# Attention scores by two 64-row halves of the array, a new order of one attention step, and a router by column groups

## What is computed

```python
qh = (layernorm(x) @ Wq + bq), kh = (ctx @ Wk + bk), vh = (ctx @ Wv + bv)   # split in 16 heads of 32
attn = softmax(qh @ kh.T / sqrt(32))                                     # 128 keys per head
x = x + tanh(g_xattn) * ((attn @ vh) @ Wo + bo)
xf = layernorm(layernorm(x)) * ln_gamma + ln_beta
logits = clip(xf @ router_w.T); two best experts, softmax of the two
y = w3[e] @ (silu(w12[e] gate @ xf) * (w12[e] up @ xf))                   # for rows within capacity
x = x + tanh(g_ffn) * sum of the two experts' y, weighted
```

## Time and profile before

| | us |
|---|---|
| median of 3 runs | 2676.12 (2672.24 to 2676.25) |
| time of the profiled execution | 2672.94 |
| its span, first to last instruction | 2671.2 |
| attention stage within it | about 482, then some 14 until the first expert matmuls |
| busy PE / DVE / ACT / POOL in the span | 2599.4 / 1362.1 / 952.6 / 422.7 |
| mean granted clock of TensorE | 0.987 |

### The profile page before, as it was taken

One profiled execution on the slowest core, in us unless ns is written; L12 is line 12 of the kernel. 1 busy time (PEld: TensorE's weight loads), 2 busy tenths in 40 slices (PEclk: granted clock), 3 DMA queues, 4 the chain that ended last, 5 costly groups with the idle time before them and its releaser, 6 DMA issues.

```text
span 2671.2 us, 40600 instructions
## 1 busy us (share of the span) xinstructions
PE 2599.4 (97%) x14168; PEld 2313.1 (87%) x14169; DVE 1362.1 (51%) x2628; ACT 952.6 (36%) x2498; POOL 422.7 (16%) x399
## 2 busy tenths in 40 slices
PE   7999999699999999999999999999999999999998
PEld 6888887699998888889888788888888999989987
DVE  5888887444444444454444444444434444445555
ACT  6777776222223222232222322322223322233343
POOL 5556565200001000010000200100001100030030
PEclk9999999799999999999999999999999999999999
DMA  8422323321114011140110511221013211142142
GB/s 332 176 97 91 107 80 112 121 88 47 47 36 110 28 43 47 34 116 24 47 47 27 124 48 71 68 71 48 24 47 71 77 47 47 47 90 102 71 128 82
DMA packets 58994, 208.37 MB, mean 78 GB/s; under 512 B 8517, under 2 KB 8797, under 8 KB 50563
## 3 DMA queue, kind: packets, MB, share of 16 engines
q1 hardware_dynamic: 42242, 175.30, 18.2%
q0 software_dynamic: 16640, 31.69, 6.2%
HBM read 145.60 MB, written 67.70 MB: 80 GB/s over the span
## 4 chain that ended last, share of the span: by engine, by line
PE 88%; DVE 4%; issue 3%; ACT 2%; POOL 1%; DMA 1%; another core or an unknown queue 1%; DVEq 0%; SPq 0%; ACTq 0%; POOLq 0%
PE bank L1601 78%; PE bank L947 6%; ACT staged L493 1%; PE bank L1047 1%; PE bank L1607 1%; PE bank L1011 1%; PE bank L1022 1%; DVE before L828 1%; PE bank L1038 0%; DVE neg_max L703 0%; POOL expert_rows L422 0%; POOL staged L389 0%; DVE xT_lo L640 0%; DVE yacc L1541 0%
## 5 line engine op out<-in xcount | busy, mean ns | idle before, releaser
L1561 DVE TENSOR_TENSOR h<-silu,bank 128x384 f32<-128x384 f32 (+2 forms) x320 | 183.8, 574 | 828.0 <-PE bank L1601 818.3
L1601 PE MATMUL bank<-slotsT_hi,early_hi 128*128 128x384 f32 (+2 forms) x1280 | 445.9, 348 | 13.1 <-issue 11.6
L1601 PE MATMUL bank<-slotsT_hi,w_hi 128*128 128x384 f32 (+2 forms) x1280 | 442.3, 346 | 3.2 <-DVE w_lo L1502 3.2
L1601 PE MATMUL bank<-slotsT_hi,early_lo 128*128 128x384 f32 (+2 forms) x1280 | 443.0, 346 | 1.7 <-issue 1.7
L1601 PE MATMUL bank<-slotsT_lo,early_hi 128*128 128x384 f32 (+2 forms) x1280 | 443.5, 346 | 0.0
L1601 PE MATMUL bank<-slotsT_lo,w_hi 128*128 128x384 f32 (+2 forms) x1280 | 442.1, 345 | 0.0
L1601 PE MATMUL bank<-slotsT_hi,w_lo 128*128 128x384 f32 (+2 forms) x1280 | 440.9, 344 | 0.0
L1469 ACT CAST h_hi<-h 128x384 fp32r<-128x384 f32 (+2 forms) x320 | 169.2, 529 | 744.0 <-DVE h L1561 741.1
L1463 ACT ACTIVATE silu<-bank 128x384 f32<-128x384 f32 (+2 forms) x320 | 162.0, 506 | 725.6 <-PE bank L1601 725.0
L1411 POOL DMA_INDIRECT out_dram<-yout,token x63 | 97.9, 1554 | 1969.4 <-ACT yout L1455 1957.9
L1541 DVE TENSOR_TENSOR yacc<-bank,yacc 128x512 f32<-128x512 f32 x464 | 316.6, 688 | 168.8 <-PE bank L1601 167.9
(11 more groups left out here) (199 smaller groups left out, 3508.9 us busy)
## 6 DMA issues: line engine op xcount, KB each, us to landing
staged<-in_moe_w_dram SPq DMA_DIRECT2D x33, 1536.0 KB
raw<-in_moe_w_dram SPq DMA_DIRECT2D x32, 1536.0 KB
xrow<-expert_rows SPq DMA_DIRECT2D x42, 520.0 KB, 8.8
expert_rows<-zeros SPq DMA_DIRECT2D x40, 520.0 KB, 7.8
xin<-in_x_dram SPq DMA_DIRECT2D x17, 512.0 KB, 3.8
xres<-in_x_dram SPq DMA_DIRECT2D x15, 512.0 KB, 3.7
out_dram<-xres SPq DMA_DIRECT2D x15, 512.0 KB
staged<-in_L_xattn_Wq_dram SPq DMA_DIRECT2D x1, 1024.0 KB, 7.2
```

Source lines behind the costliest of these rows:

```text
L1561: nc.vector.tensor_tensor(h32[q % 2][:, 0:W], silu[q % 2][:, 0:W], UB[q % 2][:, 0:W], ALU.mult)\
L1601: last = nc.tensor.matmul(out_ap, st, mv, start=(at == 0), stop=(at == n - 1))
```

## The change

Scores: `scores(n, g, b)` now makes a whole group, both token tiles. Each product is cut in two by heads: half c holds HP = 2 heads, 64 rows of the queries and keys and 256 columns of keys, and goes to bank c. For each tile t three passes, each alternating between the halves: 12 matmuls of 64 rows, 128 stationary and 256 moving columns. So bank c holds both tiles of half the heads; the scores of group g+1 wait for all exps of group g. `maxima` and `exps` go by (g, c).

Router: `rwT` is padded with zeros to 32 columns per block of features. `router(blk)` makes 4 matmuls (stationary rwT, 32 columns; moving xnT, both tiles, 256 columns), one for each block of features, to 32 partitions each. `copy_parts` on ACT copies the 128 x 256 result to SBUF, and `logits_made` multiplies it with `pick_expert`, which sums the four parts: 2 matmuls of 8 columns.

Step: PE, ACT and DVE have their pieces in a new order. On PE: scores 0, `transposes_x`, `queries(n, 1)`, `probs_T(n-1, 2)`, scores 1, `heads(n-1, 0)`, `probs_T(n-1, 3)`, `queries(n+1, 0)`, scores 2, `turn_rows`, `heads(n-1, 1)`, `router`, `probs_T(n, 0)`, `logits_made`, `attention_out(n-1, 0)`, scores 3, `positions`, `attention_out(n-1, 1)`, `probs_T(n, 1)`. In step 0 both `values_made` stand ahead of scores 1. In the tail the ACT casts of expert weights come behind the last `second_exp`. The orders on POOL and SP stay.

```diff
+            HP = HG // 2
+            parts_bank = lambda blk: l_bank(blk)[:, TB:2 * TB]
+                    nc.gpsimd.memset(rwT[:, :, :], 0.0)
...
                     def exps(blk, idx):
-                        g, t = divmod(idx, 2)
+                        g, c = divmod(idx, 2)
                         act.wait_ge(max_ready, 2 * KD * blk + idx + 1)
                         if not isinstance(blk, int) or blk > 0:
-                            act.wait_ge(pt_ready, 2 * KD * (blk - 1) + idx + 1)
-                        for hh in range(HG):
-                            h = HG * g + hh
-                            ins = nc.scalar.activation(probs[:, t, h, :], S_BANK[t][:, hh * LKV:(hh + 1) * LKV], ACT.Exp,
-                                                       bias=neg_max[:, t, h:h + 1], accum_out=sums[:, t, h:h + 1])
+                            act.wait_ge(pt_ready, 2 * KD * (blk - 1) + 2 * g + 2)
+                        for t in range(2):
+                            for hh in range(HP):
+                                h, at = HG * g + HP * c + hh, (HP * t + hh) * LKV
+                                ins = nc.scalar.activation(probs[:, t, h, :], S_BANK[c][:, at:at + LKV], ACT.Exp,
+                                                           bias=neg_max[:, t, h:h + 1], accum_out=sums[:, t, h:h + 1])
                         ins.then_inc(exp_done, 1)
...
+                    def copy_parts(blk):
+                        act.wait_ge(parts_ready, blk + 1)
+                        if not isinstance(blk, int) or blk > 0:
+                            act.wait_ge(l_ready, blk)
+                        nc.scalar.copy(parts[:, :], parts_bank(blk)).then_inc(parts_copied, 1)
...
                             pT_first(n - 1, 2)
+                        if has(n, 0):
+                            exps(n, 2)
+                        if has(n, -1):
                             a_halves(n - 1, 0)
                         if has(n, 0):
-                            exps(n, 2)
                             exps(n, 3)
...
                             a_halves(n - 1, 1)
+                        if has(n, -2):
+                            copy_parts(n - 2)
...
+                    copy_parts(LAST - 1)
+                    rows_T(LAST, (0,))
+                    second_exp(LAST - 1)
+                    rows_T(LAST, (1,))
+                    copy_parts(LAST)
+                    second_exp(LAST)
                     act.wait_ge(raw_loaded[0], 16)
                     for i in range(NU):
                         nc.scalar.copy(unit(w12_hi, w3_hi, 0, i), raw_unit(0, i)).then_inc(w_hi, 1)
-                        if i == NU // 2 - 1:
-                            rows_T(LAST, (0,))
-                            rows_T(LAST, (1,))
-                            second_exp(LAST - 1)
-                    second_exp(LAST)
...
                     def maxima(n, idx):
-                        g, t = divmod(idx, 2)
+                        g, c = divmod(idx, 2)
                         dve.wait_ge(s_ready, 2 * KD * n + idx + 1)
-                        nc.vector.tensor_reduce(neg_max[:, t, HG * g:HG * (g + 1)],
-                                                S_BANK[t][:, :].rearrange("p (h t) -> p h t", h=HG),
+                        nc.vector.tensor_reduce(neg_max[:, :, HG * g + HP * c:HG * g + HP * (c + 1)],
+                                                S_BANK[c][:, :].rearrange("p (t h k) -> p t h k", t=2, h=HP),
                                                 AX.X, ALU.max, negate=True).then_inc(max_ready, 1)
...
                             recips(n, 0)
-                            maxima(n, 2)
                             q_rest(n, 1)
+                        if has(n, 1):
+                            x_rest(n + 1)
                         if has(n, -1):
                             pT_second(n - 1, 2)
-                        if has(n, 1):
-                            x_rest(n + 1)
-                        if has(n, 0):
-                            maxima(n, 3)
                         if isinstance(n, int) and n == 0:
                             values()
+                        if has(n, 0):
+                            maxima(n, 2)
+                            maxima(n, 3)
                         if has(n, -2):
                             rows(n - 2)
...
                         if has(n, 0):
                             maxima(n, 4)
+                            maxima(n, 5)
                         if has(n, 2):
                             stats_x(n + 2)
                         if has(n, 0):
-                            maxima(n, 5)
                             recips(n, 1)
...
                             a_rest(n - 1, 1)
+                        if has(n, 0):
+                            pT_second(n, 0)
                         if has(n, -2):
                             route(n - 2)
                         if has(n, 0):
-                            maxima(n, 6)
+                            recips(n, 2)
                         if has(n, 1):
                             q_rest(n + 1, 0)
                         if has(n, 0):
-                            recips(n, 2)
-                            pT_second(n, 0)
+                            maxima(n, 6)
                             maxima(n, 7)
...
-                    def scores(n, idx, b):
-                        g, t = divmod(idx, 2)
+                    def scores(n, g, b):
                         pe.wait_ge(q_lo, KD * n + g + 1)
-                        if not isinstance(n, int) or 2 * KD * n + idx >= 2:
-                            pe.wait_ge(exp_done, 2 * KD * n + idx - 1)
-                        passes(S_BANK[t][:, :], [((qT_hi[:, g, t * P:(t + 1) * P], qT_lo[:, g, t * P:(t + 1) * P]),
-                                                  (k_hi[b][:, g, :], k_lo[b][:, g, :]))]).then_inc(s_ready, 1)
+                        if not isinstance(n, int) or KD * n + g >= 1:
+                            pe.wait_ge(exp_done, 2 * KD * n + 2 * g)
+                        for t in range(2):
+                            for i, (qs, ks) in enumerate(((qT_hi, k_hi), (qT_hi, k_lo), (qT_lo, k_hi))):
+                                for c in range(2):
+                                    rows, keys_of = slice(c * HP * DK, (c + 1) * HP * DK), slice(c * HP * LKV, (c + 1) * HP * LKV)
+                                    last = nc.tensor.matmul(S_BANK[c][:, t * HP * LKV:(t + 1) * HP * LKV],
+                                                            qs[rows, g, t * P:(t + 1) * P], ks[b][rows, g, keys_of],
+                                                            start=(i == 0), stop=(i == 2))
+                                    if t == 1 and i == 2:
+                                        last.then_inc(s_ready, 1)
...
+                    def router(blk):
+                        pe.wait_ge(xnT_ready, 2 * blk + 2)
+                        for k in range(KD):
+                            last = nc.tensor.matmul(parts_bank(blk)[DK * k:DK * (k + 1), :], rwT[:, k, :], xnT[:, :, k, :],
+                                                    start=True, stop=True)
+                        last.then_inc(parts_ready, 1)
+
+                    def logits_made(blk):
+                        pe.wait_ge(parts_copied, blk + 1)
+                        for a in range(2):
+                            last = nc.tensor.matmul(l_bank(blk)[:, a * E:(a + 1) * E], parts[:, a * P:(a + 1) * P],
+                                                    pick_expert[:, :], start=True, stop=True)
+                        last.then_inc(l_ready, 1)
...
                             scores(n, 0, b_s)
-                            scores(n, 1, b_s)
+                        if has(n, 1):
+                            if has(n, -2):
+                                pe.wait_ge(x1_ready, 2 * (n - 2) + 2)
+                            transposes_x(n + 1)
```

More of the change, by code:

```diff
@@ L553, in step @@
                             exps(n - 1, 7)
[L554 to L556 removed]
+                        if not isinstance(n, int) or n > 0:
                             if has(n, 1):
@@ L1088, in step @@
                             queries(n, 1)
-                            if isinstance(n, int) and n == 0:
-                                values_made(0)
-                            scores(n, 2, b_s)
-                        if has(n, 1):
-                            if has(n, -2):
-                                pe.wait_ge(x1_ready, 2 * (n - 2) + 2)
-                            transposes_x(n + 1)
                         if isinstance(n, int) and n == 0:
+                            values_made(0)
                             values_made(1)
```

44 lines of the change are left out of this document (19 added, 25 removed).

## The result

The kernel after takes 2692.5 us in the median of four runs (2690.5 to 2696.5), against 2676.2 for the kernel before beside it: a ratio of 1.0063, 95% interval 1.0051 to 1.0075. The forecast was 2668 and the range ended at 2690: slower, by 16 us, instead of faster by 8.6. In the profiled execution the span is 2693.9 us (its time 2696.5, which is 4.0 above the median).

The account below looks back on a forecast made before the run. PE bounds the attention step (27.07 of 27.17 us), then DVE at 24.5. Step 0 +7.9, step 1 +0.3, steps 2 to 13 -14.2, step 14 -1.1, tail -1.5: -8.6 from 2676.1, so 2668 us; range 2655 to 2690.

Parts of the forecast that it names:

- the walk: One attention step laid out anew, engine by engine, with assumed durations; it closed at 25.95 us a step.
- steps 2 to 13: Twelve attention steps going from 27.08 to 25.9 us each: -14.2 us.
- Scores: PE's score passes in attention: a group takes 0.95 us, with 0.95 to 1.65 as bounds.
- rival 1: Score passes: loads of the halves in series, group 1.65, step 27.3, 2691 us; chance 0.25 together with rival 4.
- Router: Attention step: eight head-like passes, an ACT copy and four passes; -0.85 us on PE, +0.35 on ACT.
- The step: Period of the attention loop: 25.9 us, from DVE's 24.5, a longer stall of 0.25 and 1.2 of waits.
- The base: Old attention loop: steps 2 to 13 take 27.08 us each, with PE's row of work packed.
- The term of +7.9: Step 0: PE waits for norm_x(1) and its clock falls, so the first scores of step 1 finish 7.9 us later.
- Step 14 and the tail: End of the attention stage: -1.1 us in step 14, -1.5 in step 15 and the tail.
- DVE's stall: A small DVE addition lasting until POOL's normalisation ends: 0.25 us longer per step; without the stall, 25.0 a step.
- DVE waiting longer than 1 us for maxima at group 2 or 3: Attention step: a sign that the forecast is wrong, making the exp round the bound.
- Rival 3: Attention: the stall of L828 goes and step 0 stays warm, -23 us, 2654 us; chance 0.07.

Follow-up runs that it names:

- before_third: The kernel before, unchanged, run for its trace on chip D, which had no holds: 2673.1 us.
- after_fourth: The kernel after, unchanged, on chip D without holds: 2673.6 us, ratio to the kernel before 1.0015.
- after_third: The kernel after, unchanged, on chip C without holds: 2673.5 us, ratio to the kernel before 1.0014.
- swap_third: The kernel after with queries(n, 1) put back ahead of transposes_x(n + 1) in all steps, on chip E: 2665.7 us.
- swap0: The kernel after with queries put back ahead of the transposes in step 0 alone, on chip A: 2666.9 us.
- late_scatter: The kernel after with queries ahead of transposes in all steps and POOL's four indirect DMAs moved behind norm(n - 1, 3) of the next step: 2701.6 us.

## Why the prediction was wrong, point by point

The step of the prediction that failed is the walk's second and third line: "queries(n,1) ... ends at 5.65. The ACT half is done at 6.6". I gave PE's signal to ACT no time at all beyond the pass, though the row that I cited for the length of a q half, has 1.65 us of idle time before it with a releaser that is no instruction of the core, and the earlier trace rows has 1.46 us before maxima that had their scores. I read the second as DVE's slack and did not read the first. Both are holds. They are the largest part of the miss, not all of it. The two profiled executions, before and after, give the sum term by term (their spans differ by 22.7 us where the medians differ by 16, so the miss is 31 us here and 25 in the medians):

| stretch | forecast | measured | |
|---|---|---|---|
| up to the start of step 2 | +8.2 | +11.4 | 74.02 to 85.47 |
| steps 2 to 13 | -14.2 | +5.3 | 324.9 to 330.2 |
| step 14 to the first product of expert 0 (L1601, L1629) | -2.6 | +6.2 | 103.4 to 109.6 |
| the rest | 0 | -0.2 | |

The same three stretches without holds, on chip D (before_third and after_fourth): +8.8, -6.0 and +1.7.


- **Scores.** A group of 0.95, taken from the heads' row, measured 0.90. Right, and rival 1 (loads in series, 1.65) is false, although its time of 2691 is the one that was measured: a number that comes out is no proof of its mechanism.
- **Router.** Eight passes and four, on PE as forecast; hidden in the new layout.
- **The step.** 25.9 forecast. Without holds 26.1 (after_third: (400.31 - 85.80)/12 = 26.2 over the steps 2 to 13), so the walk was off by 0.2 to 0.3. With holds 27.7: +1.6. Of the 19.4 us missing in steps 2 to 13, 15.7 are holds (330.2 against 314.5 in after_third) and 3.7 the walk's own.
- **The base.** I took 27.08 a step for the old layout; 26.7 is what its work sets, and 0.4 to 0.5 is holds. So the gain per step on a chip without holds is 0.5 to 0.6, not 1.2, and does not make up for step 0: even there the change does not pay. The forecast was 0.3% faster, and it is 0.15% slower (2673.5 and 2674.6 us against 2671.4 and 2671.1; on chip D 2673.6 against 2672.5).
- **Step 0.** PE idle from 22.2 to 28.1 and a low clock behind it, as told: eight transposes of line 998 take 1.97 us there, at a granted clock of 0.50 (28.11 to 30.10), and 1.09 in the loop. Forecast for scores(1,0) was 56.6, measured 57.95. For the start of step 2 I had 74.02 + 8.2 = 82.2; it is 85.47, and 85.80 in after_third. The term of +7.9 was mis-sized. It compared the end of the first two score tiles of step 1, before and after (49.7 and 57.5); from start to start step 1 comes 57.95 - 46.84 = 11.1 later, and then takes 27.52 us instead of 27.18, the +0.3 that was forecast. So nothing behind the scores got back the 2 us between the two ways to compare, and 1.35 us come from the later start itself. Together the two terms should have been 11.4 instead of 8.2; the exchange in step 0 gives back 7 to 9 (step 2 starts at 76.9 in swap_third and swap0, at 83.4 to 85.8 in the kernel after).
- **Step 14 and the tail.** Forecast -2.6, measured +6.2, and without holds -0.6 to +1.7 (105.1, 107.4 and 107.3 us in the kernel after against 105.7 in before_third). Step 14 alone is right without holds (25.7 us, before 26.7). That the walk to the last norm would gain did not come: from the start of step 15 it takes 30.4 to 30.7 us, before 28.6 and 30.2. Why is not shown.
- **DVE's stall** moved as the walk had it: it is now the addition of 1 in line 848, 1.88 us, ending at 359.54 with POOL's norm(n, 2) at 359.51. It hits a tensor_scalar with one SBUF source as well as the addition of two in the earlier trace rows; without holds it is line 854, 1.21 us. It was not the cause of the miss (the walk had counted a stall of this length), though it makes up 0.5 of the 1.6 us by which a step with holds is longer than one without.
- **What I said would show it.** "DVE waiting longer than 1 us for maxima at group 2 or 3" did not come; DVE waits 2.34 us for the q half instead, at a place where the walk had 1.0. A tail longer by more than 1 us did come.
- **A sum.** Rival 3's -23 us gives 2653, not 2654; nothing hangs on it.

```profile
357.66 1.88 DVE L848 TENSOR_SCALAR zsum<-e 128x2 f32<-128x2 f32 x1
...
357.59 1.92 POOL L395 TENSOR_TENSOR staged<-staged,rsums 128x1024 f32<-128x1024 f32 x1
...
28.11 1.97 PE L998 MATMUL bank<-ident,xin 128*128 128x128 f32 x8 [5.89 <-ACT xin L518]
```

## What to carry to other kernels

Before a row's duration is used, read what stands in its brackets: a wait whose releaser had ended long before is a latency of its own, and a new order decides whether it lies in slack or on the chain. Where a trace shows such holds, keep the signals on which a step hangs away from the moments at which another engine issues indirect DMAs, or at least do not put work with a late input (the transposes) ahead of work that is ready (the queries). Compare kernels on more than one chip where they differ by less than a per cent: here the same pair of kernels differs by 0.15% on chip C and by 0.68% on chip B.

## What the runs showed of the hardware

- On one of five chips PE's semaphore updates are held beside POOL's indirect DMAs, by up to 2.7 us, and most come out 0.7 to 0.9 us after the end of the last one's instruction. The late ones end 2.6 to 5.6 us after the start of the first of the four; earlier ones were on time, and so were ACT's and DVE's as far as can be told. In the traces with holds the record of the semaphores lacks updates in the same stretch (13 to 22 of ACT's and of DVE's in each, against none to one in the others). On the other four chips no update of PE is late by more than 0.06 us, with the same programs; the two profiles of the first result, whose chip I don't know, have the holds. What differs between the chips, and whether it is the indirect form of the DMA that does it or the transfers, is open. By the medians on the chips, the kernel before is 3 to 5 us slower with holds and the kernel after 17 to 18.
- Matmuls on the two halves of 64 rows run two at a time, loads included: 12 passes of 256 columns in 0.90 us instead of 1.60.
- A small DVE instruction beside POOL's normalisation of 128 x 1024 can last until that one ends: 1.88 us instead of 0.16 for a 128x2 tensor_scalar with one source in SBUF.
- An indirect DMA of 128 rows occupies POOL for 1.0 us with 0.3 to the next, and in late_scatter the source of the last of four was free for its writer 2.8 us after the instruction had ended.
